# AdaLN cross-attention on one core: the products with the values as 48 half-height matmuls per tile instead of 24 full-height ones

## The reference

```python
xq = _ada_ln(x_q, t_vec, Wss_q, bss_q)          # (16, 1024, 512)
xkv = _ada_ln(x_kv, t_vec, Wss_kv, bss_kv)      # (16, 64, 512)
q = (xq @ Wq + bq).reshape(B, Lq, nh, dh)
kv = (xkv @ Wkv + bkv).reshape(B, Lkv, 2, nh, dh)
k = kv[:, :, 0]
v = kv[:, :, 1]
scores = jnp.einsum('bqhd,bkhd->bhqk', q, k) / jnp.sqrt(jnp.float32(dh))
attn = jax.nn.softmax(scores, axis=-1)
out = jnp.einsum('bhqk,bkhd->bqhd', attn, v).reshape(B, Lq, H)
return x_q + (out @ Wp + bp)
```

## Time and profile before

| | |
|---|---|
| median of 3 runs | 1210.9 us (1210.82 to 1213.61) |
| the profiled execution | 1211.32 us |
| its span, first to last instruction | 1209.5 us |
| PE busy | 1180.0 us, 98% |
| DVE busy | 980.4 us, 81% |
| ACT, POOL busy | 703.0 and 706.0 us, 58% each |
| mean granted clock of TensorE | 0.992 of full speed |

### The profile page before, as it was taken

How to read it: one execution, slowest core, us unless ns; L and a number is a source line. 1 busy time by engine, 2 the same in 40 slices (tenths; PEclk the granted TensorE clock), 3 DMA queues, 4 the chain that set the end, 5 groups by cost and what they waited for, 6 DMA issues and landing times.

```text
span 1209.5 us, 33685 instructions
## 1 busy us (share of the span) xinstructions
PE 1180.0 (98%) x11584; PEld 772.5 (64%) x11584; DVE 980.4 (81%) x2052; ACT 703.0 (58%) x1176; POOL 706.0 (58%) x948
## 2 busy tenths in 40 slices
PE   7799899999999999999999999999999999999997
PEld 2675666666666666666666666666666666666664
DVE  4787888888888888888888888888888888888875
ACT  1466556665656556665656565565656565565653
POOL 1553656657474756666575756666565656656434
PEclk9799999999999999999999999999999999999999
DMA  8110222332223232232323222323223222222222
GB/s 330 62 44 27 88 89 97 89 95 87 98 84 99 86 101 86 96 95 88 95 87 95 87 95 87 101 85 100 87 95 92 90 95 87 95 87 84 65 71 80
DMA packets 59866, 111.93 MB, mean 93 GB/s; under 512 B 6412, under 2 KB 6440, under 8 KB 59832
## 3 DMA queue, kind: packets, MB, share of 16 engines
q1 hardware_dynamic: 41400, 77.92, 21.2%
q10 hardware_dynamic: 18432, 33.56, 7.3%
HBM read 77.90 MB, written 33.55 MB: 92 GB/s over the span
## 4 chain that ended last, share of the span: by engine, by line
issue 46%; POOL 37%; POOLq 2%; DVE 0%; DVEq 0%
POOL xr L414 12%; POOL xh L381 7%; POOL w_lo L420 5%; POOL w_tmp L404 5%; POOL rstd L369 2%; POOL xr L390 2%; POOLq L221 2%; POOL nmv L365 2%; POOL veps L367 2%; POOL cur_sc L399 0%; POOLq L244 0%; POOLq L40 0%; POOLq L399 0%; DVE mv L812 0%; DVE oT_lo L827 0%
## 5 line engine op out<-in xcount | busy, mean ns | idle before, releaser
L553 ACT ACTIVATE q_hi<-ps_q,cur_bq 128x512 f16<-128x512 f32 x126 | 86.6, 687 | 268.0 <-PE ps_q L1113 230.6
L365 POOL TENSOR_TENSOR nmv<-mv,sign 128x2 f32<-128x2 f32 x128 | 27.0, 211 | 352.0 <-DVE mv L812 352.0
L820 DVE TENSOR_TENSOR xT_lo<-ps_t,xT_hi 128x512 f16<-128x512 f32 x128 | 88.5, 692 | 162.4 <-ACT xT_hi L494 162.4
L414 POOL TENSOR_TENSOR xr<-y,xr 128x512 f32<-128x512 f32 x128 | 163.1, 1275 | 46.1 <-ACT y L519 46.1
L390 POOL TENSOR_TENSOR xr<-xr,bp_row 128x512 f32<-128x512 f32 x128 | 163.1, 1274 | 13.1 <-POOL rstd L369 6.9
L876 DVE TENSOR_TENSOR pt_lo<-ps_t,pt_hi 128x512 f16<-128x512 f32 x256 | 164.7, 685 | 3.7 <-ACT pt_hi L543 3.5
L868 DVE TENSOR_TENSOR pr<-ps_s,mx 128x512 f32<-128x512 f32 x256 | 163.7, 681 | 0.0
L856 DVE TENSOR_REDUCE mx<-ps_s 128x8 f32<-128x512 f32 x256 | 158.8, 662 | 0.1
L494 ACT CAST xT_hi<-ps_t 128x512 f16<-128x512 f32 x128 | 75.0, 586 | 142.2 <-PE ps_t L1096 142.0
L584 ACT ACTIVATE pr<-pr,exp_scale 128x1024 f32<-128x1024 f32 x128 | 149.6, 1169 | 6.2 <-DVE pr L868 6.2
L543 ACT CAST pt_hi<-ps_t 128x512 f16<-128x512 f32 x256 | 136.3, 588 | 5.3 <-PE ps_t L1149 5.3
(11 more groups left out here) (160 smaller groups left out, 2323.7 us busy)
## 6 DMA issues: line engine op xcount, KB each, us to landing
x_in<-in_x_dram SPq DMA_DIRECT2D x128, 256.0 KB, 2.6
xr<-in_x_dram SPq DMA_DIRECT2D x128, 256.0 KB, 2.6
out_dram<-xr ACTq DMA_DIRECT2D x128, 256.0 KB, 2.2
raw<-in_L_xcond_Wss_kv_dram SPq DMA_DIRECT2D x4, 512.0 KB, 5.4
cx<-in_ctx_dram SPq DMA_DIRECT2D x1, 2048.0 KB, 12.4
raw<-in_L_xcond_Wss_q_dram SPq DMA_DIRECT2D x4, 512.0 KB, 13.4
raw<-in_L_xcond_Wkv_dram SPq DMA_DIRECT2D x2, 1024.0 KB, 15.7
wq<-in_L_xcond_Wq_dram SPq DMA_DIRECT2D x1, 1024.0 KB, 16.9
```

Source lines behind the costliest of these rows:

```text
L414: pool.tensor_tensor(xr[:, s, :], y[:, off % 2, :], xr[:, s, :], ALU.add).then_inc(y_ready, 1)
```

## The change

The products of a pair's two heads become two matmuls, each on 64 rows of the array, `e = 0` into one bank of `ps_v` and `e = 1` into the other, alternating. Their moving operand has 33 columns (32 where it is the lo part, which needs no column of ones). `vb` loses its zero blocks and one of its dimensions, and is filled by one copy of 128 rows. The banks now hold even heads and odd heads, so the two DVE operations on `ps_v` address them otherwise, and they wait for both halves of `weigh`.

```diff
-        vb = sb("vb", [P, 2, PAIRS, 2, VC], F16)
+        vb = sb("vb", [P, 2, PAIRS, VC], F16)
...
-            pool.memset(vb[:, :, :, :, :], 0.0).then_inc(zeros_ready, 1)
-            pool.wait_ge(zeros_ready, 1)
-            for par in range(2):
-                rows = slice(LKV * par, LKV * (par + 1))
-                pool.memset(vb[rows, 0, :, par, DH:VC], 1.0).then_inc(bd_ready, 1)
-
-                pool.wait_ge(bd_ready, 2 + par)
+            pool.memset(vb[:, 0, :, DH:VC], 1.0).then_inc(bd_ready, 1)
...
-                for part in range(2):
-                    for par in range(2):
-                        rows = slice(LKV * par, LKV * (par + 1))
-                        act.copy(vb[rows, part, :, par, 0:DH], v_all[rows, part, b, :, :]).then_inc(vb_done, 1)
+                act.copy(vb[:, :, :, 0:DH], v_all[:, :, b, :, :]).then_inc(vb_done, 1)
...
-                    for h in range(2):
-                        wait(dve, pv_mm, 2 * unit(b, off) + h + 1)
-                        dve.reciprocal(rden[:, HALF * h:HALF * (h + 1)], ps_v[:, h, DH:HALF * VC:VC])\
+                    wait(dve, pv_mm, 2 * upto(b, off))
+                    for e in range(2):
+                        dve.reciprocal(rden[:, HALF * e:HALF * (e + 1)], ps_v[:, e, DH:HALF * VC:VC])\
...
                     for g in range(4):
-                        pair = 4 * h + g
-                        dst = ps_v[:, h, 2 * VC * g:2 * VC * (g + 1)]
-                        for n, (pt, part) in enumerate(((pt_hi, 0), (pt_hi, 1), (pt_lo, 0))):
-                            last = pe.matmul(dst, pt[:, pair, :],
-                                             vb[:, part, 2 * g + h, :, :].rearrange("p h c -> p (h c)"),
-                                             start=(n == 0), stop=(n == 2))
+                        pair, c = 4 * h + g, 2 * g + h
+                        for n, (pt, part, w) in enumerate(((pt_hi, 0, VC), (pt_hi, 1, DH), (pt_lo, 0, VC))):
+                            for e in range(2):
+                                rows = slice(LKV * e, LKV * (e + 1))
+                                last = pe.matmul(ps_v[:, e, VC * c:VC * c + w], pt[rows, pair, :],
+                                                 vb[rows, part, c, 0:w], start=(n == 0), stop=(n == 2))
                     last.then_inc(pv_mm, 1)
```

More of the change, by code:

```diff
@@ L120, in adaln_cross_attention @@
         o_slot = o[:].rearrange("p h d -> p (h d)")
-        o_pairs = o[:].rearrange("p (m e r) d -> p e m r d", e=2, r=2)
+        o_pairs = o[:].rearrange("p (c e) d -> p e c d", e=2)
         brow = o_slot[0:7 * KC, 0:P]
@@ L640, in prime @@
                         act.wait_ge(k_ready, KC)
-                        act.wait_ge(bd_ready, 3)
+                        act.wait_ge(bd_ready, 2)
                         key_blocks(0)
@@ L843, in normalise_o @@
                 wait(dve, o_turned, unit(b, off))
[L844 to L848, removed]
+                for e in range(2):
+                    dve.tensor_tensor(o_pairs[:, e],
+                                      ps_v[:, e, 0:HALF * VC].rearrange("p (c v) -> p c v", v=VC)[:, :, 0:DH],
+                                      rden[:, HALF * e:HALF * (e + 1)].unsqueeze(2).to_broadcast([P, HALF, DH]),
                                       ALU.mult)\
@@ L1158, in weigh @@
                 if off % PER == 0:
-                    wait(pe, vb_done, 4 * (b + off // PER + 1))
+                    wait(pe, vb_done, b + off // PER + 1)
                 wait(pe, o_done, 2 * unit(b, off))
```

## The result

The changed kernel takes 1311.63 us (median of 4, 1309.49 to 1313.09) against 1211.04 before: the ratio is 1.0824, with a 95% interval of 1.0803 to 1.0845. It is slower by 100 us, more than the range of the prediction allows.

A forecast was written before the change was run, and what follows sets the result against it. The prediction took PE, busy 98% of the span, to bound the kernel. From 1211.32 us it took 16 for the pairs and added 34 for refetches at branches, other terms 0: 1229 us, range 1190 to 1262.

The forecast's parts named there:

- the price of a branch with a refetch: At the loop's 13 branches back, PE waits for a missing instruction packet: 2.6 us each, +34 us (9 to 44).
- The first wait: At the branch back, PE waits for the body's first packet: 2.2 us less 0.4 of queued `weigh`, 1.8 us.
- The second wait: After one `score` of 0.65 us, PE waits for the body's next packet if only then asked for: another 1.55 us.
- The dearest refetch that was allowed for: Upper end of the refetch term over 13 branches back, at 3.35 us each: 44 us.
- Pairs of 33 columns: In `weigh`, 24 pair steps of 25 ns replace steps of 30.4 ns: 0.127 us a unit, -16 us in all.
- The way to it from f32 loads: Pair price in `weigh` from f32 transposes: 62 ns apart, less a 53 ns load, plus a 15 ns f16 load: 24.
- the 9 ns called handover: In the f32 transposes, load and handover were said to cost 9 ns beyond the 53 ns load.
- The serial rival: In `weigh`, halves don't overlap when this short: 48 steps of 25 ns, +60 us, 1272 us (1306 with refetch); chance 0.10.
- The change of shape: Loss of 0.09 us between full-height and half-height matmuls moves from behind `weigh` to ahead of it: 0.
- DVE, semaphores, vb: Reciprocals waiting for both halves, `weigh` needing `pt_lo`, and filling `vb` by one copy: no effect on the time, 0.
- Nine packets and seven: PE's loop body grows from seven instruction packets, which stay, to nine, held likelier than not to be refetched.
- The branch without a refetch: Rival in which nine packets stay: branches back cost 2 us more in all, 1197 us; chance 0.31.

The follow-up runs named there:

- e7: The changed kernel with 60 columns a head in place of 33 in the first and third term of `weigh`: 1321.69 us in one run.
- e6: The changed kernel with `weigh` not alternating, twelve matmuls on one half of the array, then twelve on the other: 1346.27 us in one run.
- e9: Kernel before with new products in 85 units (0 to 4 of each loop batch), an old `weigh` ahead of the branch, fulfilled waits behind long matmuls: 1200.75 us, ratio 0.9918.
- e4: Kernel before with new products in five of eight units, some 165 fulfilled waits more ahead of the loop, body in seven packets: 1207.84 us, ratio 0.9968.
- e5: Kernel before with new products in 86 units (3 to 7 of each loop batch), 77 fulfilled waits ahead of the loop, body in seven packets: 1206.22 us, ratio 0.9965.
- e2: Kernel before, matmuls untouched, with 48 fulfilled-wait instructions more a unit on PE, making its program as long as the changed one: 1342.69 us in one run.
- e8: Kernel before, matmuls untouched, with 24 fulfilled-wait instructions more a unit on PE, loop body in seven packets: 1214.67 us in one run.
- e3: Kernel before with new products in five of eight units, old `vb` layout kept, loop body in eight packets: 1274.19 us, ratio 1.0512.
- e1: The changed kernel with 75 fulfilled-wait instructions more on PE ahead of the loop, so its body covers eight packets, not nine: 1271.59 us, ratio 1.0497.

## Why the prediction was wrong

**The direction and the mechanism were right, one term was a third of its size.** The step that failed is the price of a branch with a refetch, "So 1.8 to 3.35 us a branch ... I take 2.6: +34 us". It measured 8.8 us and 114 in all. Three things make the difference. The first wait is 3.9 us at the branch shown above and 4.4 in the mean, not 1.8: a fetch was priced at the 2.2 us of the fastest data transfer listed, but the packet needs 0.8 us to start, 1.2 to move, and PE goes on only 1.9 us after that. The moving alone was priced right, at 1.1. The second wait was left to a choice between none and 1.55 us by taking the middle; it is there, at 2.3 us (2.5 in the mean), in the first `score`, where the prediction had placed it. And the clock was left out: it falls to its lower level behind the waits, 1.9 us more in `project` here, 1.6 in the mean, and 0.3 in `score`. The dearest refetch that was allowed for, 44 us, was built on the same 2.2 us.

**Pairs of 33 columns: right.** 25 ns predicted, 25 measured. A unit gained 0.123 us against 0.127. The way to it from f32 loads (62 ns less 53, plus 15) holds as a number, but in part by luck. No row shows the 53 ns by itself: the f32 transposes start 62 ns apart with 16 columns and 109 with 128, so by these rows some 55 ns do not depend on the columns, and the 9 ns called handover are mostly the 16 columns. e7 shows that the number is a floor for short matmuls. The serial rival is excluded by the timeline, and e6 shows what it was made of. Here the Trainium skill, "TensorEngine Tiling (Array Packing)", section Instruction Overhead, is borne out: its 60 cycles, 25 ns at 2.4 GHz, are what one matmul holds its half of the array for (25 ns in e6), and not what each instruction costs the engine (48 in 0.62 us).

**The change of shape: right,** 0.09 us moved from one side of `weigh` to the other, nothing gained.

**DVE, semaphores, vb: right.** PE has no gap outside the branches in any of the kernels that fit (879.94 of 880 us in e9). e4, e5 and e9 keep the four copies and the zero blocks and lose nothing by it.

**Nine packets and seven: right, the border was open.** e2 and e8 show that length alone makes the loss in the loop, e3 and e4 that it starts at eight packets. The Trainium skill, "Runtime: NRT & Kernel Launch", section Instruction fetch mechanics, has room for eight 16 KiB blocks. The runs are stricter: seven stay and eight do not. That one place is taken by the packet asked for ahead of the body's end would explain it, and agrees with the nine packets a pass of e1; no run isolated it.

**The branch without a refetch:** the rival had "at most 0.4 us more, 13 times, 5 us" and took 2. e5 measured 0.42 and 5.5.

## What to carry to other kernels

Count the instructions of a hardware loop's body on TensorE, each matmul as two, before splitting matmuls: past seven packets of 256 every pass pays 6 to 9 us here, and where the loop begins within a packet decides as well. Two alternating half-height matmuls cost 25 ns a pair here at 33 columns and 27 at 60, so they beat one full-height matmul of 66 columns (30 ns) by a sixth, no more. And keep long work ahead of a branch back: it hides the branch.

## What the runs showed beside

- A fulfilled wait, as an instruction of its own on PE, costs 108 ns where nothing is queued ahead (40 of them put the first matmul at 5.96 us, 98 at 12.21 us), and nothing behind long matmuls (e8 in the loop).
- In e6 matmuls of two stages ran at once on the two halves of the array: `score` matmuls start at 613.46 and 613.52 us between those of `weigh` that stand ahead of them in the program.
- A stretch of 4.5 us with 0.78 us of PE work was followed by some 7 us mostly at the lower clock. In e1, behind its single wait of 3.7 us, the granted clock from 610.8 to 618 us was 0.61.
